# Adding the routed results of each token in memory, four sums per token, instead of storing eight rows and adding them on VectorE

## What is computed

```python
x = x + slot_attention(cond, ctx, layernorm(x), ...)        # three rounds
h = layernorm(x).reshape(-1, 256)                           # 2048 tokens
scores = sigmoid(h @ gate_w.T)
tki = top_k(masked(scores + gate_bias), 8)[1]               # 8 experts per token
combine = one_hot(tki) * (2.5 * weights of the 8, normed)
g = silu(einsum('th,eih->tei', h, w_gate))
u = einsum('th,eih->tei', h, w_up)
routed = einsum('tei,ehi->th', g * u * combine[:, :, None], w_down)
shared = silu(h @ sh_gate.T) * (h @ sh_up.T) @ sh_down.T
x = x + routed + shared
```

## Time and profile before

| | us |
|---|---|
| time, median of 3 runs | 629.0 (626.36 to 634.15) |
| the profiled execution's own time | 632.99 |
| its span, first to last instruction | 631.7 |
| PE busy | 562.0 (89%) |
| DVE busy | 414.6 (66%) |
| POOL busy | 374.3 (59%) |
| ACT busy | 358.4 (57%) |

### The profile page before, as it was taken

One profiled execution on the slowest core, in us unless ns is written; L12 is line 12 of the kernel. 1 busy time (PEld: TensorE's weight loads), 2 busy tenths in 40 slices (PEclk: granted clock), 3 DMA queues, 4 the chain that ended last, 5 costly groups with the idle time before them and its releaser, 6 DMA issues.

```text
span 631.7 us, 11423 instructions
## 1 busy us (share of the span) xinstructions
PE 562.0 (89%) x2621; PEld 416.7 (66%) x2621; DVE 414.6 (66%) x1616; ACT 358.4 (57%) x945; POOL 374.3 (59%) x420
## 2 busy tenths in 40 slices
PE   3999989997999788996997999999999999999830
PEld 2765537763676445664675888888888888877720
DVE  7956946696659996886765444444544444788767
ACT  3748657867586738624402656566566666655520
POOL 4313401662074348788777777777777777777750
PEclk9979979997999979995998999999999999999975
DMA  8994000000000012283349999766666667999777
GB/s 276 396 397 177 1 1 2 0 1 0 1 1 2 0 54 103 105 319 117 126 157 304 325 331 317 228 200 221 215 203 208 213 197 226 330 386 375 271 282 296
DMA packets 58238, 116.28 MB, mean 184 GB/s; under 512 B 8747, under 2 KB 41567, under 8 KB 56127
## 3 DMA queue, kind: packets, MB, share of 16 engines
q1 hardware_dynamic: 43823, 72.65, 35.0%
q0 software_dynamic: 13776, 41.83, 17.3%
q10 hardware_dynamic: 576, 1.08, 0.5%
HBM read 61.29 MB, written 54.23 MB: 183 GB/s over the span
## 4 chain that ended last, share of the span: by engine, by line
PE 64%; DVE 11%; POOL 9%; ACT 6%; DMA 6%; issue 4%; SPq 0%; DVEq 0%; POOLq 0%; ACTq 0%
PE ps L1947 20%; PE ps L1964 10%; PE ps L1603 5%; PE ps L1937 5%; POOL xrows L578 5%; PE ps L1588 5%; PE ps L1627 3%; PE ps L1614 3%; DVE tokrow L716 3%; PE ps L1957 2%; PE ps L1574 2%; POOL yrows L671 2%; DMA arena<-yrows 2%; ACT hat L1338 2%; PE ps L1723 2%
## 5 line engine op out<-in xcount | busy, mean ns | idle before, releaser
L1947 PE MATMUL ps<-arena,mats 128*128 x636 | 165.7, 384 | 0.5 <-ACT mats L1389 0.3
L578 POOL DMA_INDIRECT xrows<-tokrow,place_of x128 | 129.4, 1011 | 44.4 <-issue 37.8
L1241 DVE TENSOR_TENSOR mats<-ps,mats 128x128 f32<-128x128 f32 x159 | 46.3, 291 | 111.2 <-ACT mats L1396 109.2
L1947 PEld LDWEIGHTS ps<-arena,mats 128*128 128x128 f32 x636 | 109.5, 192 | 10.2 <-issue 1.6
L1964 PE MATMUL ps<-arena,mats 128*128 x318 | 96.1, 384 | 1.0 <-DVE mats L1248 1.0
L1396 ACT ACTIVATE mats<-ps 128x128 f32<-128x128 f32 x159 | 44.1, 277 | 58.8 <-PE ps L1947 58.8
L671 POOL DMA_INDIRECT yrows<-hatT,mats x64 | 62.3, 973 | 19.5 <-issue 13.7
L514 POOL TENSOR_SCALAR var_eps<-variance 128x4 f32<-128x4 f32 x24 | 5.3, 221 | 105.1 <-ACT hat L1330 104.9
L1389 ACT COPY mats<-ps 128x256 f32<-128x256 f32 x159 | 57.9, 365 | 13.5 <-PE ps L1937 13.3
L1330 ACT ACTIVATE hat<-tokrow,total 128x256 f32<-128x256 f32 x96 | 47.6, 499 | 18.7 <-DVE tokrow L716 10.1
L1964 PEld LDWEIGHTS ps<-arena,mats 128*128 128x128 f32 x318 | 48.0, 191 | 14.4 <-issue 1.9
(11 more groups left out here) (224 smaller groups left out, 1072.1 us busy)
## 6 DMA issues: line engine op xcount, KB each, us to landing
hat<-xrows SPq DMA_DIRECT2D x81, 160.0 KB, 3.3
rows<-xrows SPq DMA_DIRECT2D x78, 160.0 KB, 3.5
arena<-in_experts SPq DMA_DIRECT2D x4, 1920.0 KB, 16.8
hat<-yrows SPq DMA_DIRECT2D x6, 1024.0 KB, 7.6
tokrow<-yrows SPq DMA_DIRECT2D x6, 1024.0 KB
xrows<-padrow SPq DMA_DIRECT2D x32, 160.0 KB
xrows<-padrow SPq DMA_DIRECT2D x1, 4960.0 KB, 29.5
arena<-in_experts SPq DMA_DIRECT2D x2, 2304.0 KB, 16.7
```

The lines of the kernel that those rows point to most:

```text
L578: gp.indirect_dma_start(out=xrows[:, :], out_offset=bass.IndirectOffsetOnAxis(ap=place_of[:, g, k:k + 1], axis=0), in_=tokrow[:, g, :], in ...
L1947: mm = te.matmul(bank(6 + u)[:, 0:2 * I], turned_row[u][:, dc * P:(dc + 1) * P], arena[:, dc * D:(E - 1) * WCOL + (dc + 1) * D][:, bass.ds ...
```

## The change

`yrows` now holds 4 sums per token instead of 8 rows. A scatter adds its 128 rows to what stands there (`compute_op=ALU.add`); scatter n adds to the token's sum number n mod 4. Since two adds to the same sum must not overlap, scatter n first waits until scatter n-4 has landed (`summed_up`), one semaphore for each of the four sums. SP fills `yrows` with zeros beforehand (8.7 MB), and the first four scatters wait for that (`cleared`). A token's number is now the same for all experts, so the scan goes and `DST` is written once as a constant. The way back loads 4 rows per token (512 KB a group) and needs one addition of 128x512 less three: `add_halves`, then `add_last`. `copy_out` waits for the one scatter that last used its buffer. The DMAs on POOL keep their number and order.

```diff
-YROWS = TOPK * B * S + TILES * P
+SUMS = 4
+YROWS = SUMS * (B * S + P)
...
+            sy.dma_start(yrows.rearrange("(p n) d -> p n d", p=P),
+                         padrow[:, 0:D].rearrange("p (o d) -> p o d", o=1).to_broadcast([P, YROWS // P, D])
+                         ).then_inc(cleared, 16)
...
-                for u in range(YGROUPS):
-                    sy.wait_ge(scattered[u], 16 * sum(n // YGROUP % YGROUPS == u for n in range(tiles)))
+                for a in range(SUMS):
+                    sy.wait_ge(summed_up[a], 16 * len(range(a, tiles, SUMS)))
...
-                gp.memset(keep[:, :], 1.0).then_inc(pool_seq, 1)
-                gp.wait_ge(pool_seq, seq.add())
-                gp.memset(keep.rearrange("p (t e) -> p t e", e=E)[:, :, 0:1], 0.0).then_inc(consts, 1)
-                gp.iota(token_id[:, :], pattern=[[P * TOPK, B * T]], base=-1, channel_multiplier=TOPK,
+
+                gp.iota(tokrow[:, :, DST:ROW], pattern=[[P * SUMS, B * T], [0, E]], base=0, channel_multiplier=SUMS,
...
             def scatter(n):
                 gp.wait_ge(y_ready, n + 1)
                 gp.wait_ge(aimed, n // GROUP + 1)
+                if n < SUMS:
+                    gp.wait_ge(cleared, 16)
+                else:
+                    gp.wait_ge(summed_up[n % SUMS], 16 * (n // SUMS))
                 gp.indirect_dma_start(
                     out=yrows[:, :], out_offset=bass.IndirectOffsetOnAxis(ap=scatter_to[:, n:n + 1], axis=0),
-                    in_=ybuf[y_place(n)], in_offset=None).then_inc(scattered[n // YGROUP % YGROUPS], 16)
+                    in_=ybuf[y_place(n)], in_offset=None, compute_op=ALU.add).then_inc(summed_up[n % SUMS], 16)
...
-                step(ve.tensor_tensor_scan(count_upto[:, :], keep[:, :], masked[:, ts, :].rearrange("p t e -> p (t e)"),
-                                           0.0, ALU.mult, ALU.add))
-                ve.scalar_tensor_tensor(out=tokrow[:, ts, DST:ROW],
...
-                ve.tensor_tensor(scatter_to[:, n:n + GROUP], own[:, n:n + GROUP, 1], nowhere[:, n:n + GROUP], ALU.min
-                                 ).then_inc(aimed, 1)
+                ve.scalar_tensor_tensor(out=scatter_to[:, n:n + GROUP], in0=own[:, n:n + GROUP, 1],
+                                        scalar=nowhere[:, 0:1], in1=sum_of[:, n:n + GROUP], op0=ALU.min, op1=ALU.add
+                                        ).then_inc(aimed, 1)
...
-                add_half(last_sums[g], 0).then_inc(dve_seq, 1)
-                seq.add()
-                step(add_half(last_sums[g], 1))
-                step(add_quarters(last_sums[g]))
+                step(add_halves(last_sums[g]))
                 step(add_last(last_sums[g]))
...
-                if n >= YFIRST and y_last(n) % YGROUP == 0:
-                    u = y_last(n) // YGROUP
-                    ac.wait_ge(scattered[u % YGROUPS], 16 * YGROUP * (u // YGROUPS + 1))
+                if n >= YFIRST:
+                    u = y_last(n)
+                    ac.wait_ge(summed_up[u % SUMS], 16 * (u // SUMS + 1))
```

## The result

| | before | after |
|---|---|---|
| time, median, us | 629.95 (626.36 to 634.15) | 722.44 (721.47 to 727.27) |
| ratio | | 1.148, 95% interval 1.139 to 1.157 |
| span of the profiled execution, us | 631.7 | 720.2 |
| POOL busy, us | 374.3 | 469.8 |
| PE busy, us | 562.0 | 561.7 |

A forecast was written before the change was run, and what follows sets the result against it. POOL, issuing without a pause, was taken as the bound: 631.7 - 6.9 (tail) - 0.7 (start) - 0.8 (back loads) + 31.8 (scatter issue) = 655.1 us span, put at 652 us on the median; range 617 to 705 us.

The forecast's parts named there:

- What bounds the kernel: POOL issues indirect DMAs without a pause, ending within 3.3 us of PE; longer scatters reach the end almost in full.
- The scatter's issue: On POOL, each adding scatter takes 0.2 us longer to issue, bounds 0 and +0.96; 159 x 0.2 = 31.8 us.
- The new wait: On POOL, scatter n waits for n-4; an add lands in 4.9 us, under four periods of 5.06 us: cost 0.
- the margin of 0.2 us: On POOL, what four issue periods of 5.06 us leave over a 4.9 us landing if issue time does not grow.
- The tail: After the last scatter lands, halved loads and shorter sums take 9.7 us instead of 16.6: gain 6.9 us.
- Before the first dispatch: The scan and add ahead of the first dispatch go, so POOL starts earlier: gain 0.7 us.
- Clearing: SP's 8.7 MB of zeros take 52 us by size, over some 200 us before the first scatter: cost 0.
- DMA engines: A scatter takes 0.344 us of all 16 engines, unchanged if adding equals copying, 0.69 by the skill's rule; sum unchanged.
- rival 1: The addition is a flag: POOL keeps its 1.265 us period, 620.6 us, not slower; chance 0.34.
- Rival 2: Scatter chain of four becomes the bound: period a quarter of the landing, 671 us at 6.5, 723 at 8; chance 0.18.

The follow-up runs named there:

- the run that only adds: The kernel before, eight rows per token and no scatter waiting for another, with each scatter adding to zero-filled rows: 722.8 us, ratio 1.153.
- The forms: The kernel before with zero fill, scatters in turn adding or writing 128, 64, 32 rows: issue 1.60, 1.43, 1.33 us adding; 0.97, 0.94, 0.89 us writing.

## Why the prediction was wrong, step by step

- **What bounds the kernel**: right. POOL issues without a pause, and what was added to a scatter came out at the end almost in full: 159 x 0.60 = 95 us, and the run that only adds lost 92.
- **The scatter's issue, "I take +0.2 us"**: this step failed. It measured +0.60 us (+0.65 in the mixed stretch). The bounds, 0 and +0.96, held it; the value was chosen by counting addresses, which gives +0.48 at most, and the range was cut at +0.5. The forms show why counting addresses misleads: some 0.38 us come with the addition itself, whatever the rows. With +0.60 the sum of the prediction would have been 623.3 + 95.4 = 718.7 for the span, where 720.2 was measured. That it comes so near is in part luck: the profiled execution began its scatters 8.2 us early, which makes up for the chain and the longer tail.
- **The new wait, "the cost is 0"**: too low. The chain costs 6.3 us in the changed kernel and 7 to 9 with plain writes. The middle landing came out as sized, 4.9 us in the run that only adds, though not for the reason given: with nothing beside it an add lands after 3.7 us. What was missing is the stretch in which sums are loaded, where landings take far longer (7.9 us in the median of that run, at most 9.6), and the 0.76 us from a landing to the next start, against which the margin of 0.2 us was none. POOL issues without a pause, so what it loses there is never made good. The prediction's own rows had a hint of it: 2.5 us as the median of dispatches, and 9.9 us as the longest.
- **The tail**: 9.7 us from landing to last sum was forecast, 10.5 measured; the gain is 6.1 us and not 6.9. The first load took 3.7 us, as forecast; but the third sum still waited for its load, and starts 2.17 us after the second instead of 1.52.
- **Before the first dispatch, 0.7 us**: can't be told; the start of the dispatches varies by 8 us between executions.
- **Clearing**: free, as said; it took 35 us to land and not 52.
- **DMA engines**: the row of before, taken as copying, gave 0.344 us a scatter, and it is 1.00. The factor of two that the Trainium skill ("Collectives: The Full Stack", under the bandwidth ceiling) gives for an addition against a copy was on the right side, but it is too small here: the trace has 2.9, with 144 packets instead of 48. It still did not set the time, since a scatter only comes every 1.93 us, and DMA_INDIRECT is 1.56 us with these engines 95% busy (440 to 520 us) as well as at the end, with no loads beside it.
- **The rivals**: rival 1 is refuted by the 1.56 us. Rival 2, the chain as the bound, gave 723 us for a landing of 8 us, which is the time that was measured, and is wrong all the same: its sign was to be an unchanged DMA_INDIRECT with idle time before it, and the reverse is on the timeline. Its side effects (SP, DVE and PE stopped at the first load of sums, without cost) came, from POOL's lateness.

## What to carry to other kernels

An operation that moves work from an engine with slack into a queue that issues without a pause is paid in that queue, once per instruction. Where no row prices its issue, run the range up to the bound; and multiply by the count first, since here a tenth of a microsecond was 16 us. A chain of n transfers under way costs nothing only while n issue periods cover the longest landing in the company that it will have, not the middle one, and the restart behind it, here 0.76 us.

## What the runs showed of the hardware that was not expected

- An indirect DMA that adds costs POOL 1.56 us for 128 rows of 1 KB against 0.96 us for one that writes, and 1.33 against 0.89 us for 32 rows.
- It makes 144 packets instead of 48 (a scatter has 128 rows), takes 1.00 instead of 0.344 us of the 16 engines in 440 to 520 us, and lands after 3.7 instead of 2.5 us with no loads beside it.
- A DMA on POOL that has to wait for a landing starts 0.76 us after it (two sums, adding), where the gap is 0.30 us when there is nothing to wait for.
- The first dispatch starts between 220.4 and 228.8 us in the profiled executions, and it varies for one and the same kernel too (float16 results: 220.75, 223.67 and 228.81). The mean granted TensorE clock of 0 to 180 us goes with it: 0.94 where it starts at 228.6 and 228.8, 0.97 where it starts at 223.5 to 224.6, 0.99 where it starts at 220.4. The execution of the kernel before that the prediction was built on was one of the late ones.
- On two of the chips the kernel before takes 738 to 740 us, with an expert loop that begins late and then sets POOL's pace; six adding sums cost 3.2 and 3.3% there.
